# A graph convolution in which the centring of the layer norm is parted, one row maximum is moved ahead of the variance, and the mixing weights are multiplied only where they are not zero

## The reference

```python
s = softmax(left(xt) @ xt.T / sqrt(CT))            # per batch 512 x 512, left = xt @ W1_s @ W2_s, rank 10
h = einsum('bnm,bmct->bnct', s * A[None], xt)      # spread over the nodes
g = einsum('bnct,cf->bnft', h, W_gcn)
y = relu(conv2d(swap(g), tcn_w, pad 1 in time) + x_res)   # three taps: t-1, t, t+1
mu = mean(y over its 16 channels); var = mean((y - mu)**2)
z = (y - mu) / sqrt(var + 1e-5) * ln_g + ln_b
```

## Time and profile before

| | |
|---|---|
| median of three runs | 1548.05 us (1540.19 to 1551.75) |
| the profiled execution | 1554.25 us, its span 1552.4 us |
| mean granted TensorE clock | 0.911 |
| busy, share of the span | PE 86%, PEld 72%, DVE 62%, ACT 44%, POOL 38% |
| graph convolution, first layer | from about 132 to 427 us |
| graph convolution, second layer | from about 1098 to 1393 us |

### The profile page before, as it was taken

How to read it: one execution, slowest core, us unless ns; L and a number is a source line. 1 busy time by engine, 2 the same in 40 slices (tenths; PEclk the granted TensorE clock), 3 DMA queues, 4 the chain that set the end, 5 groups by cost and what they waited for, 6 DMA issues and landing times. The chain is left out here.

```text
span 1552.4 us, 25779 instructions
## 1 busy us (share of the span) xinstructions
PE 1331.2 (86%) x8330; PEld 1121.0 (72%) x8330; DVE 969.0 (62%) x2091; ACT 686.6 (44%) x1195; POOL 592.6 (38%) x904
## 2 busy tenths in 40 slices
PE   6787999999494899999999994676899999947997
PEld 5686888888493788888888873566698888833554
DVE  4412788888667545444544433646378888856895
ACT  5432454555274333233323323522245454526996
POOL 1100266566620464575457431100036566560000
PEclk8788999999895899999999995578799999978999
DMA  7371011111074354665456526884111111100111
GB/s 242 119 217 42 22 53 49 51 51 41 21 241 151 118 109 110 139 116 110 109 137 121 87 34 180 287 260 127 42 32 52 41 52 50 51 11 11 42 52 61
DMA packets 86321, 148.81 MB, mean 96 GB/s; under 512 B 13907, under 2 KB 31971, under 8 KB 86247
## 3 DMA queue, kind: packets, MB, share of 16 engines
q1 hardware_dynamic: 63975, 103.78, 21.6%
q0 software_dynamic: 16384, 31.51, 11.7%
q10 hardware_dynamic: 5888, 12.59, 2.3%
HBM read 94.32 MB, written 53.51 MB: 95 GB/s over the span
## 5 line engine op out<-in xcount | busy, mean ns | idle before, releaser
L935 PE MATMUL g_y<-L_z,L_pt 128*128 128x192 f32 x1024 | 197.2, 337 | 1.6 <-ACT L_pt L1151 0.5
L935 PEld LDWEIGHTS g_y<-L_z,L_pt 128*128 128x128 f32 x1024 | 167.3, 194 | 6.9 <-ACT L_pt L1151 6.9
L1097 POOL TENSOR_TENSOR L_xr<-L_xr,L_lnb 128x192 f32<-128x192 f32 x128 | 105.6, 852 | 169.1 <-DMA L_xr<-x 89.5
L1492 POOL DMA_INDIRECT sums<-x_yo,x_places x64 | 102.9, 1608 | 135.8 <-ACT x_yo L1731 125.8
L1143 ACT ACTIVATE L_e<-g_s,L_nm 128x512 f32<-128x512 f32 x128 | 87.9, 687 | 134.2 <-DVE L_nm L983 133.5
L1104 POOL TENSOR_TENSOR L_t<-L_rstd 128x48 f32<-128x48 f32 x96 | 29.1, 303 | 203.2 <-DVE L_rstd L1039 198.2
L920 PE MATMUL g_t<-s_ident,L_p 128*128 128x128 f32 x512 | 79.6, 279 | 31.5 <-DVE L_p L992 31.4
L1621 DVE TENSOR_TENSOR x_mid<-ex_g,x_sig 128x480 f32<-128x480 f32 (+1 forms) x48 | 31.4, 654 | 119.7 <-ACT x_sig L1722 119.7
L992 DVE SCALAR_TENSOR_TENSOR L_p<-L_e,L_rl,L_adj 128x512 f32<-128x512 f32 x128 | 99.2, 775 | 4.5
L983 DVE TENSOR_REDUCE L_nm<-g_s 128x1 f32<-128x512 f32 x128 | 87.5, 683 | 20.5 <-PE g_s L912 19.7
L920 PEld LDWEIGHTS g_t<-s_ident,L_p 128*128 128x128 f32 x512 | 61.9, 142 | 48.4 <-DVE L_p L992 44.8
(11 more groups left out here) (351 smaller groups left out, 3495.6 us busy)
## 6 DMA issues: line engine op xcount, KB each, us to landing
L_xnT<-xn_rows SPq DMA_DIRECT2D x48, 384.0 KB, 3.4
xn_rows<-L_xnT SPq DMA_DIRECT2D x54, 192.0 KB, 3.1
L_xr<-in_x SPq DMA_DIRECT2D x24, 384.0 KB, 3.1
L_raw<-xn_rows SPq DMA_DIRECT2D x16, 384.0 KB, 5.9
L_xr<-x SPq DMA_DIRECT2D x16, 384.0 KB, 3.1
out_x<-ff_yo SPq DMA_DIRECT2D x16, 384.0 KB, 2.6
s_gu<-in_Wg SPq DMA_DIRECT2D x8, 704.0 KB
s_gu<-in_Wu SPq DMA_DIRECT2D x8, 704.0 KB
```

The costliest lines, as they stand in the source:

```text
L935: last = nc.tensor.matmul(out, pt[k % 2][:, P * c:P * c + P], z[q][:, c, :], start=False, stop=(c == NK - 1))
L1097: last = nc.gpsimd.tensor_tensor(v_, v_, gain(s.lnb), ALU.add)
L1492: nc.gpsimd.indirect_dma_start(sums, row(places[e % 2][:, 1, t:t + 1]), yo[t % 4][:, :], None, compute_op=ALU.add).then_inc(sent[t % 4], 16)
```

## The change

VectorE's `centre` is cut in two: `means` (sum and scale) stays in its place, and `centre` (the subtraction) moves behind `row_probs(b, 2)` and `row_max(b, 3)`. `row_max(b + 1, 0)` moves from behind the variance to ahead of it.

The matrix `wm` and its product `kw` get a new order of columns: the mixing columns of times 0 to 5, the projection columns, the mixing columns of times 6 to 11. The rows of half 0 (times 0 to 5) have mixing weights only for times 0 to 6, those of half 1 only for times 5 to 11; all else is zero. With the new order the columns that each half reaches are one stretch, and `kron_weights` multiplies only these. `conv_slab` reads the mixing columns in two pieces, `projections` the 64 columns from 96 on; the buffers `wm`, `kw0` and `kw1` get 316 columns instead of 254, and `ConvWeights.mix` writes the mixing columns as two stretches of 96, with one more dimension in its access patterns.

```diff
+NKW = CT + NPROJ            # 254
+SPAN = HALF + NPROJ         # 96 + 62 = 158
+REACH = SPAN + O            # 174
...
     def mix(self, h, dt):
-        mask = s.tmask[:, h, dt, :].unsqueeze(2).to_broadcast([HALF, T, O])
-        tap = rows(self.mixed[:, h, O * dt:O * dt + O], T)
-        mix = s.wm[:, h, NPROJ:NPROJ + CT].rearrange("p (t o) -> p t o", t=T)
+        halves = lambda x: x.rearrange("p (a t) -> p a t", a=2)
+        mask = halves(s.tmask[:, h, dt, :]).unsqueeze(3).to_broadcast([HALF, 2, TH, O])
+        tap = self.mixed[:, h, O * dt:O * dt + O].unsqueeze(1).unsqueeze(1).to_broadcast([HALF, 2, TH, O])
+        mix = halves(s.wm[:, h, :])[:, :, 0:HALF].rearrange("p a (t o) -> p a t o", t=TH)
...
                     for ho in range(2):
-                        for h in range(2):
-                            last = nc.tensor.matmul(psz[0:HALF, 0, (NPROJ + CT) * ho:(NPROJ + CT) * (ho + 1)],
-                                                    kron[q][0:HALF, h, HALF * ho:HALF * ho + HALF], s.wm[:, h, :],
-                                                    start=(h == 0), stop=(h == 1))
+                        for h, lo, hi, start, stop in ((0, 0, REACH, True, False), (1, HALF - O, REACH, False, True),
+                                                       (1, REACH, NKW, True, True)):
+                            last = nc.tensor.matmul(psz[0:HALF, 0, NKW * ho + lo:NKW * ho + hi],
+                                                    kron[q][0:HALF, h, HALF * ho:HALF * ho + HALF], s.wm[:, h, lo:hi],
+                                                    start=start, stop=stop)
                     last.then_inc(kw_done, 1)
...
+                def taps(w, h):
+
+                    return w[0:HALF, h, :].rearrange("p (a x) -> p a x", a=2)[:, :, 0:HALF]
...
-                                                    xnT[q][0:HALF, h, P * k:P * k + P], kw[q][0:HALF, h, NPROJ:],
+                                                    xnT[q][0:HALF, h, P * k:P * k + P], taps(kw[q], h),
...
                     if softmax:
                         row_max(b, 2)
                     if norm:
-                        centre(b - 1, r)
+                        means(b - 1, r)
                     if softmax:
                         row_probs(b, 2)
                         row_max(b, 3)
+                    if norm:
+                        centre(b - 1, r)
                     if project:
                         split_uv(b + 1, r)
                     if softmax:
                         row_probs(b, 3)
                     if total:
                         residual(b - 2, q)
+                    if project:
+                        row_max(b + 1, 0)
                     if norm:
                         variance(b - 1, r)
                     if project:
-                        row_max(b + 1, 0)
                         row_probs(b + 1, 0)
                         row_max(b + 1, 1)
```

More of the change, by code:

```diff
@@ L171, in conv_loads @@
         (bias2[:, 0:O], p("tcn_b")), (bias2[:, O:2 * O], p("res_b")),
-        (s.wm[:, :, 0:NPROJ], p("ws").rearrange("(h p) r -> p h r", p=HALF)),
+        (s.wm[:, :, HALF:SPAN], p("ws").rearrange("(h p) r -> p h r", p=HALF)),
         (s.wc[:, :, :, :], p("wc").rearrange("(k p) (x r) -> p k x r", p=P, r=PROJ)),
@@ L217, in prepare @@
         dve.wait_ge(self.loaded, 16 * CONV_LOADS)
-        nc.vector.tensor_scalar(s.wm[:, :, 0:KR], s.wm[:, :, 0:KR], 1.0 / float(np.sqrt(np.float32(CT))), None, ALU.mult)
+        nc.vector.tensor_scalar(s.wm[:, :, HALF:HALF + KR], s.wm[:, :, HALF:HALF + KR], 1.0 / float(np.sqrt(np.float32(CT))), None, ALU.mult)
         nc.vector.tensor_copy(self.lhs_g.rearrange("p (t c) -> p t c", t=T),
@@ L250, in mix @@
         rows = lambda x, n: x.unsqueeze(1).to_broadcast([HALF, n, O])
-        mask = s.tmask[:, h, dt, :].unsqueeze(2).to_broadcast([HALF, T, O])
-        tap = rows(self.mixed[:, h, O * dt:O * dt + O], T)
-        mix = s.wm[:, h, NPROJ:NPROJ + CT].rearrange("p (t o) -> p t o", t=T)
-        tm = self.small[0:HALF, 480:480 + CT].rearrange("p (t o) -> p t o", t=T)
+        halves = lambda x: x.rearrange("p (a t) -> p a t", a=2)
+        mask = halves(s.tmask[:, h, dt, :]).unsqueeze(3).to_broadcast([HALF, 2, TH, O])
+        tap = self.mixed[:, h, O * dt:O * dt + O].unsqueeze(1).unsqueeze(1).to_broadcast([HALF, 2, TH, O])
+        mix = halves(s.wm[:, h, :])[:, :, 0:HALF].rearrange("p a (t o) -> p a t o", t=TH)
+        tm = self.small[0:HALF, 480:480 + CT].rearrange("p (a t o) -> p a t o", a=2, t=TH)
         if dt == 0:
@@ L891, in projections @@
                         for j in range(2):
-                            last = nc.tensor.matmul(psz[UV * j:UV * j + UV, 1, 0:NODES], kw[q][0:HALF, h, 0:UV],
+                            last = nc.tensor.matmul(psz[UV * j:UV * j + UV, 1, 0:NODES], kw[q][0:HALF, h, HALF:HALF + UV],
                                                     xnT[q][0:HALF, h, NODES * j:NODES * j + NODES],
@@ L1018, in split_uv, with means @@
                     last.then_inc(uv_sb, 1)
-                def centre(b, q):
+                def means(b, q):
                     step.begin(b * NORM_STEPS)
@@ L1025, in centre @@
                     step(nc.vector.tensor_scalar(s.mu[:, :, :], s.mu[:, :, :], 1.0 / O, None, ALU.mult))
+                def centre(b, q):
                     dve.wait_ge(gained, free(b, 2))
@@ L1124, in copy_kw @@
                     act.wait_ge(z_done, free(b, 2))
-                    nc.scalar.activation(kw[q][0:HALF, :, :],
-                                         psz[0:HALF, 0, 0:2 * (NPROJ + CT)].rearrange("p (h x) -> p h x", h=2),
+                    nc.scalar.activation(kw[q][0:HALF, :, 0:NKW],
+                                         psz[0:HALF, 0, 0:2 * NKW].rearrange("p (h x) -> p h x", h=2),
                                          ACT.Copy).then_inc(kw_sb, 1)
@@ L2327, in conv_buffers @@
     s.wt = sb("wt", [P, NK, C, PROJ])
-    s.wm = sb("wm", [HALF, 2, NPROJ + CT])
+    s.wm = sb("wm", [HALF, 2, 2 * SPAN])
     s.res = sb("res", [P, 2, HALF])
@@ L2359, in conv_buffers @@
     s.k1 = sb("k1", [P, 2, CT])
-    s.kw0 = sb("kw0", [P, 2, NPROJ + CT])
-    s.kw1 = sb("kw1", [P, 2, NPROJ + CT])
+    s.kw0 = sb("kw0", [P, 2, 2 * SPAN])
+    s.kw1 = sb("kw1", [P, 2, 2 * SPAN])
     s.u0 = sb("u0", [P, N], F32R)
```

## The result

The changed kernel takes **1602.6 us** (median of four, 1596.63 to 1613.04), the one before 1545.5: 1.0375 times as long, 95% interval 1.0299 to 1.0451. It is slower, as forecast, but by 57 us instead of 22, and so outside the range of 1545 to 1588. The profiled execution took 1607.7 us, its span 1605.9.

A forecast was written before the change was run, and what follows sets the result against it. Bound: VectorE up to the variance, GpSimd's Newton chain, the divide, 16.37 us a turn. A layer: 13 x (0.60 + 0.20) + 1.5 - 0.84 = 11.1 us; two layers 22 us on the median 1548.05 give 1570 us, range 1545 to 1588.

The forecast's parts named there:

- the row maximum: VectorE, `row_max(b+1,0)` ahead of the variance: makes variance, Newton chain and divide later, +0.60 us a turn.
- its wait for the scores: VectorE's moved row maximum waits for the next batch's first scores: 0.20 us a turn, ends 0 and 1.07.
- the stretch of the Newton chain: GpSimd, from the last variance instruction to the divide: taken unchanged at 5.53 us, ends 4.53 us and 0.5 more.
- their sum is the same, so `split_uv` and the variance start no earlier: VectorE, subtraction moved behind `row_probs(b,2)` and `row_max(b,3)`: only the order changes, 0 on the path.
- The mixing weights: TensorE, `kron_weights`: 12 rows in 1.18 to 1.43 us instead of 8 in 1.72, worth 0 in full turns.
- The filling turns: First turn with a norm in each layer: the variance comes later, +1.1 to +2.1 us, taken +1.5.
- The tail: Last turn with softmax in each layer: the subtraction covers VectorE's wait behind `row_max(15,3)`, -0.84 us.
- TensorE then waits elsewhere in the turn: TensorE, parted centring: `L_p` comes 1.32 us earlier and removes its 0.86 us stall; the wait elsewhere was given no cost.
- Rival 3: VectorE's moved row maximum: scores come late, wait 1.07 us, a turn costs 1.67, 1593 us; chance 0.08.
- TensorE as the bound: Graph convolutions: TensorE bounds the turns, each gives back 1.3 us, 1514 us; chance 0.08.
- The shorter chain: GpSimd's Newton chain falls below 4.73 us; at 4.53 each turn wins 0.2, 1544 us; chance 0.14.
- The longer chain: GpSimd's Newton chain is blocked 0.3 us more by VectorE's multiply, a turn +1.10, 1578 us; chance 0.12.

The follow-up runs named there:

- newton2_after: The changed kernel with two Newton steps instead of three in GpSimd's loop; 1532.1 us, 0.9889 of the kernel before.
- only_rowmax: The kernel before with one edit, `row_max(b+1,0)` ahead of the variance; 1626.4 us, 1.0518 times the kernel before.
- no_rowmax: The changed kernel with `row_max(b+1,0)` back behind the variance, parted centring and mixing weights kept; 1553.2 us, 1.0025 times the kernel before.
- awake_full_turns: The changed kernel with eight dummy matmuls ahead of the projections, only in turns from 2 on, not the two that fill; 1582.3 us.
- only_centre: The kernel before with one edit, the subtraction of the centring moved behind `row_max(b,3)`; 1552.2 us, 1.0031 times the kernel before.
- awake: The changed kernel with eight 128 x 128 dummy matmuls (16 rows) ahead of the projections of each turn with a softmax; 1588.6 us.
- variance_early: The changed kernel with the variance right behind `split_uv`, the Kronecker matrix behind `row_max(b+1,0)` and the divide ahead of `row_probs(b+1,1)`; 1554.4 us.
- kw_first: The changed kernel with one edit on ScalarE, `copy_kw(b+1)` ahead of `row_exp(b,2)`; 1587.1 us, 1.0247 times the kernel before.

## Why the prediction was wrong

**Right: the path and the cause.** The turn closes over VectorE, the Newton chain and the divide (newton2_after), `row_max(b+1,0)` ahead of the variance lengthens it (only_rowmax, no_rowmax), and it costs per turn at full clock 25.1 / 26 = 0.97 us in awake_full_turns against 0.80 forecast, near the upper end of the prediction's turn (+1.0).

**The terms.** In the turn at full clock shown above: the row maximum 0.61 us (1357.22 to 1357.83, forecast 0.60); its wait for the scores 0.2 us (1357.22 less 1356.14 and the 0.87 us from the start of the residual to the next start, as before; forecast 0.20); the stretch of the Newton chain 5.33 us, 0.20 shorter than before, but 5.54 in the turn behind it and 5.50 to 5.58 in 19 of the 26, so the forecast of 0 fits most turns. The term that was missing on the path is the 0.2 us that an instruction loses right behind the moved subtraction: "their sum is the same, so `split_uv` and the variance start no earlier" was too kind, they start later. With it the usual turn of 17.45 us is accounted for to 0.1 us (16.37 + 0.80 + 0.2). The mixing weights are 1.26 us, inside 1.18 to 1.43, and worth nothing, as said. The setup instructions with a fourth dimension are 20, not 24, and took 0.35 us each before and after, not 0.25; the 0 taken for them is right. The filling turns cost 1.0 and 1.6 us (1.5 forecast). The tail gained 0.3 to 0.4 us instead of 0.84. So the path comes to 25.1 + 2.6 - 0.7 = 27 us over both layers, where the sum had 22.

**The step that failed** is the sentence "TensorE then waits elsewhere in the turn": the sum puts what TensorE's added wait does at nothing. I had read the granted clock of 1.00 as given for every turn. The divide, made late by the row maximum that the sum prices at "+0.60 us a turn", makes TensorE wait 1.95 us for `L_kw`; the clock fell behind this wait in part of the turns, and 26 us of the 51 that the turns lost are that. With the wait filled by dummy matmuls the clock stays at 1.00, and what is left is 1582.3 us, inside the range. The sentence stands beside the parted centring, but the missing term belongs to the row maximum: only_rowmax loses the clock without that centring, only_centre and no_rowmax keep it.

No rival had this. Rival 3 (scores late, 1.07 us) has the right place for VectorE's wait (now line 992), but its cause was TensorE's order, not its clock. The prediction's own sign for it, a wait of over 0.5 us there, is met in the turns with the clock fallen (3.03 us above); only the turns at 1.00, with 0.2 us, tell the two apart.

**The other rivals.** TensorE as the bound (1514) is out: awake adds 16 rows a turn, and the turns get shorter. The shorter chain (1544) needed 4.73 us; it is 5.20 at the least. The longer chain (1578) did not come in the changed kernel (5.20 to 5.58 us): the first multiply blocks one GpSimd operation to 0.61 us, as one before. GpSimd of the changed kernel in order of time:

```profile
1359.62 0.27 POOL L1119 TENSOR_TENSOR L_t<-L_rstd 128x48 f32<-128x48 f32 x1 [5.50 <-DVE L_rstd L1051]
1359.96 0.61 POOL L1120 TENSOR_TENSOR L_t<-L_t,L_hvar 128x48 f32<-128x48 f32 x1
```

In variance_early it did come; GpSimd there, under the multiply and the residual behind it:

```profile
289.87 0.61 POOL L1120 TENSOR_TENSOR L_t<-L_t,L_hvar 128x48 f32<-128x48 f32 x1
290.56 0.88 POOL L1121 TENSOR_TENSOR L_t<-s_c,L_t 128x48 f32<-128x48 f32 x1
```

Later in the same chain these two operations take 0.28 or 0.29 us; the whole chain is 5.88 us. The Trainium skill's rule ("SBUF — State Buffer", "Summary: rules for kernel authors": the second of the two to issue blocks until the first is finished) agrees with the trace; in the changed kernel it agrees as well, but changed nothing in the sum.

## What to carry to other kernels

In a loop over several engines, add up the one path that closes a turn before moving a step: a step that "hides a wait" costs its full length when the wait lay beside that path and the step now lies on it. Where TensorE isn't the bound, its slack is part of the design: ask how much longer a new order makes it wait, and price the turn at the lower clock too. Moving work from ahead of a long hand-over to behind it can pay, until the work behind is as long as the hand-over: of the two orders tried with the variance early, one gained 0.7% and the other nothing.

## What was not expected of the hardware

The granted clock fell in turns whose longest TensorE wait was 1.98 us, and not in others with nearly the same wait: in the first layer three turns of 13 were at 1.00 throughout, in the second nine. The changed kernel and kw_first, in which a wait of nearly the same length lies elsewhere, spent 65 and 34 us of the turns at the lower level; only_rowmax, with two shorter waits, 55 us. What tells these turns apart was not found.
